# Two transformer layers: how the softmax maximum's blocks are spread over the first attention's steps at a token chunk's end

## The reference

```python
# layer 0, 16 heads of 16 features
S = jnp.einsum('hid,hjd->hij', K, Q) * SCALE
delta = idx[:, None] - idx[None, :]
decay = jnp.where(delta < 0, 0.0, -delta.astype(jnp.float32) ** ALPHA)
S = jnp.where(delta < 0, -jnp.inf, S) + decay
C = jax.nn.softmax(S, axis=-1)
attn = jnp.einsum('hij,hjd->hid', C, V)
...
x = x + ga * attention(h);  h = _layernorm(x) * (1 + cb) + sb;  x = x + gb * ffn(h)
```

## Time and profile before

| | us |
|---|---|
| median of three runs | 1557.49 |
| the profiled execution | 1556.74 |
| its span | 1554.9 |
| PE busy | 1407.1 (90%) |
| VectorE busy | 1202.4 (77%) |
| ScalarE busy | 1039.5 (67%) |
| block reductions (L1766), 832 | 914.0 |
| exponentials (L1501), 1664 | 846.2 |

### The profile page before, as it was taken

The page is one execution under the profiler, slowest core; times in us unless marked ns, Lnnn a source line. Parts: engine busy times, 40 slices in busy tenths (PEclk is TensorE's granted clock), DMA queues, the critical chain, the costliest instruction groups (busy, mean ns, idle before and its releaser), DMA issues.

```text
span 1554.9 us, 35205 instructions
## 1 busy us (share of the span) xinstructions
PE 1407.1 (90%) x13320; PEld 592.7 (38%) x13320; DVE 1202.4 (77%) x1592; ACT 1039.5 (67%) x2052; POOL 316.9 (20%) x376
## 2 busy tenths in 40 slices
PE   6878888899899998986899989999999989999998
PEld 5543333333333354442233332333333333236675
DVE  5687897898786044888899979997999779816766
ACT  2245675777688832231798978998988888984443
POOL 2401231000000032223500018300400040046225
PEclk9988999999999999996799999999999999999999
DMA  7721121011000003222200200000000000012455
GB/s 225 143 47 36 49 70 34 27 33 44 5 2 2 1 15 69 48 48 59 84 7 7 53 7 7 7 7 7 7 7 7 7 2 2 2 59 86 144 151 149
DMA packets 56867, 68.51 MB, mean 44 GB/s; under 512 B 9819, under 2 KB 52379, under 8 KB 55963
## 3 DMA queue, kind: packets, MB, share of 16 engines
q1 hardware_dynamic: 53635, 57.87, 14.2%
q0 software_dynamic: 3072, 8.39, 1.8%
HBM read 45.26 MB, written 26.74 MB: 46 GB/s over the span
## 4 chain that ended last, share of the span: by engine, by line
issue 40%; PE 33%; DVE 12%; POOL 8%; ACT 4%; DMA 3%; SPq 1%; POOLq 0%; DVEq 0%; ACTq 0%
DVE mpart L1766 8%; PE psum L1254 6%; PE psum L1229 4%; ACT probs L1501 3%; PE psum L1297 3%; PE psum L1198 3%; PE psum L1306 3%; PE psum L1325 3%; PE psum L1371 2%; PE psum L1390 1%; POOL ffn_w L972 1%; PE psum L1158 1%; DMA key_region<-in_w_up 1%; POOL key_region L984 1%; POOL key_region L986 1%
## 5 line engine op out<-in xcount | busy, mean ns | idle before, releaser
L1766 DVE TENSOR_REDUCE mpart<-psum 128x2 f32<-128x1024 f32 (+2 forms) x832 | 914.0, 1155 | 107.4 <-PE psum L1198 88.6
L1501 ACT ACTIVATE probs<-psum 128x512 f32<-128x512 f32 (+3 forms) x1664 | 846.2, 573 | 174.1 <-PE psum L1229 96.3
L1254 PE MATMUL psum<-probs,v_region 128*17 128x256 f32 (+2 forms) x6144 | 496.4, 396 | 11.6 <-ACT out_sb L1516 7.9
L1198 PE MATMUL psum<-key_region,row_region 50*128 50x512 f16 (+3 forms) x1664 | 322.8, 380 | 64.7 <-DVE mpart L1766 50.3
L1229 PE MATMUL psum<-row_region,key_region 52*128 52x512 f16 (+3 forms) x1664 | 350.9, 380 | 16.0 <-ACT probs L1501 13.3
L1229 PEld LDWEIGHTS psum<-row_region,key_region 52*128 52x128 f16 x1664 | 97.7, 93 | 354.7 <-ACT probs L1501 292.4
L1254 PEld LDWEIGHTS psum<-probs,v_region 128*17 128x17 f32 x6144 | 102.7, 95 | 206.9 <-issue 103.4
L1198 PEld LDWEIGHTS psum<-key_region,row_region 50*128 50x128 f16 x1664 | 94.5, 94 | 166.9 <-DVE mpart L1766 98.6
L928 POOL TENSOR_SCALAR vare<-mv 128x4 f32<-128x4 f32 x16 | 3.7, 232 | 646.4 <-DVE mv L1680 646.4
L1536 ACT ACTIVATE probs<-psum,gate_s 128x512 f32<-128x512 f32 (+1 forms) x24 | 16.4, 683 | 73.1 <-PE psum L1297 73.1
L1037 POOL TENSOR_TENSOR key_region<-probs,key_region 128x512 f16<-128x512 f32 (+1 forms) x24 | 28.0, 1166 | 154.1 <-ACT key_region L1545 154.0
(11 more groups left out here) (191 smaller groups left out, 1330.5 us busy)
## 6 DMA issues: line engine op xcount, KB each, us to landing
parts<-key_region SPq DMA_DIRECT2D x32, 256.0 KB, 2.7
key_region<-parts SPq DMA_DIRECT2D x48, 128.0 KB, 4.2
sorted_x<-in_zero SPq DMA_DIRECT2D x46, 128.0 KB, 2.5
key_region<-sorted_x SPq DMA_DIRECT2D x46, 128.0 KB, 2.1
sorted_y<-key_region SPq DMA_DIRECT2D x46, 128.0 KB, 1.8
row_region<-parts SPq DMA_DIRECT2D x144, 32.0 KB
key_region<-in_wmod SPq DMA_DIRECT2D x2, 1536.0 KB, 11.5
x_sb<-in_x SPq DMA_DIRECT2D x4, 512.0 KB, 8.3
```

Of the source, the lines that this page charges most:

```text
L1198: mm = pe.matmul(bank(b + par)[:, 0:w], rows[at, g, hp, r * P:(r + 1) * P], keys[at, g * HP + hp, q * CH:q * CH + w], start=True, stop=not ...
L1254: mm = pe.matmul(psum[32 * h:32 * h + VW, SUM_BANK, lo:hi], v_sb[:, jt, g * HG + h, :], probs[:, (S0[y] + s) % 2, h, lo:hi], start=(jt == ...
L1501: nc.scalar.activation(probs[:, (S0[y] + s) % 2, 2 * hp + par, off:CH], psum[:, e % 3, off:CH], ACT.Exp, scale=SCALES[y]).then_inc(s_p, 1)
L1766: V.tensor_reduce(mpart[:, n % NG, at:at + 2, q:q + 1], psum[:, b:b + 2, 0:w], AX.X, ALU.max).then_inc(drained(*item)[0], 1)
```

## The change

The factors become one dictionary for each attention. The second attention's is the old one; the first attention, which had none, gets none of its share in step 3 and half in steps 4 and 6 of units 4, 8 and 12.

```diff
--- before.py
+++ after.py
@@ -114,7 +114,7 @@
 
 def spread_blocks(y, queue):
 
-    work = [step_work(y, n, k) * (CHUNK_END.get(k, 1) if y and n and n % NG == 0 else 1) for n in range(NU) for k in range(steps_of(y, n))]
+    work = [step_work(y, n, k) * (CHUNK_END[y].get(k, 1) if n and n % NG == 0 else 1) for n in range(NU) for k in range(steps_of(y, n))]
     queue = list(queue)
     given, ready = [[] for _ in work], {}
     due = {n: sum(block_work(y, b) for b in queue if b[2] <= n) for n in range(NU)}
@@ -159,7 +159,7 @@
 
 
 
-CHUNK_END = {2: 0.5, 3: 0.0, 4: 0.5, 5: 0.5, 6: 0.25}
+CHUNK_END = ({3: 0.0, 4: 0.5, 6: 0.5}, {2: 0.5, 3: 0.0, 4: 0.5, 5: 0.5, 6: 0.25})
 RT_PIECES = 6
 DP_PIECES = 4
```

## The result

The changed kernel took 1564.12 us (median of 21 runs, 1558.32 to 1572.85), the kernel before 1557.55 (21 runs): a ratio of 1.0038, interval 1.0025 to 1.005, or 5.9 us more by the ratio. The forecast was 1555.5 with a range of 1549.5 to 1560.5. A second measurement (after_again, 12 runs against 35) gave 1.0020, 1.0004 to 1.0036, or 3 us. So the change costs 3 to 6 us by these two measurements.

What follows compares the result with a forecast made beforehand. VectorE and ScalarE were held almost in balance, with the chunk ends bound by a chain across engines. Ends give 7.5 us, landing costs 5.5: 1557.49 - 2.0 = 1555.5 us, range 1549.5 to 1560.5.

Steps and rivals of the forecast that it cites:

- The order: First attention's block table: 14 blocks leave steps 3 to 7 of units 4, 8 and 12; orders equal from step 105.
- What the ends give back: Steps 3 to 7 of units 4, 8 and 12 get shorter by 7.5 us, between 6.1 and 9.0.
- The 1.1 us for a block in step 6: Price per block from unit 12's step 6, first attention against second: 7.4 against 5.2 us for two blocks.
- The move of unit 9's transposed maximum: Unit 9's transpose of the maximum goes from unit 8's step 5 to 6: put at 0, between -1 and +1.
- What landing costs: Of 12.9 us of VectorE time leaving the ends and landing elsewhere, 5.5 us paid, kept between 0 and 12.9.
- The two unit 9 places named as free: Unit 9's steps 0 and 11 take 0.8 and 1.13 us of blocks free, since VectorE is partly idle there.
- the 6.4 us that went to steps with two or three blocks: Rest of the landing, mostly in units 5, 6, 9 and 10; with it, 5.5 us were taken as paid.
- 27 us of idle VectorE time: VectorE's idle time in the three stretches behind the ends, 6.7 + 11.5 + 8.8; basis for the landing's lower bound, nothing.
- B: Rival: step 3's hidden blocks are paid at 1.13 where they land in saturated steps; slower, 1564.3 us; chance 0.12.
- A: Rival: landing is free, VectorE's 27 us of idle time take all of it; 1550.3 us; chance 0.30.
- C: Rival: units 4 and 12 keep or get three blocks in step 5, step 6's low clock stays; 1558.5 us; chance 0.18.
- thinner ends would invite the low clock: Fear from the skill's clock rule: taking matmuls from steps where PE waits invites it; forecast read the rows the other way.

Runs made afterwards that it cites:

- after_again: The changed kernel, unaltered, measured once more with a second profile: ratio 1.0020 (1.0004 to 1.0036) against the kernel before; first attention 457.8 us.
- twice_between: Kernel before, with 8 full blocks in steps between the ends reduced twice, the second result unread: 1.0047 (1.0029 to 1.0064), 7.3 us slower.
- before_four: Kernel before, blocks pulled forward so unit 4 step 2, unit 5 step 2 and unit 6 step 1 have four: 1.0044 (1.0025 to 1.0062), 6.9 us slower.
- steps 4 and 6 alone: Kernel before with steps 4 and 6 halved and step 3 keeping its full share: 0.9973, 4.2 us faster; measured again 0.9978, 3.4 us faster.

## Why the prediction was wrong

**The order.** The table of blocks, worked out by the planner's rule, was right, and the two orders are one from step 105 on.

**What the ends give back** was forecast as 7.5 us (6.1 to 9.0) and measured as 7.1 and 8.5. The sum held, its parts did not. Step 3 gave 2.0 where 0.8 was forecast (1.3 of it in unit 4, where I had used unit 12's 0.1 for a block), and step 4 gave 2.6 where 0.9 was. Step 5 gave 4.1 us, though I had it 0.85 longer, and step 6 became longer, by 1.5 and 0.1 us in the two profiles, though I had it 5.5 shorter. That these errors cancel to the forecast sum is luck. The 1.1 us for a block in step 6 was for the most part the low clock in the window that I read it from the earlier trace rows: doubled blocks cost nothing there. I read one window at 0.77 against one at 1.00 and laid the whole difference to the blocks, though I had named the clock in the next paragraph. And a table by single steps misses what a block does to the step behind it, as unit 4's step 5 shows. The move of unit 9's transposed maximum from unit 8's step 5 to its step 6, which I had put at 0, goes with the two largest differences within the ends: unit 8's step 5 is 2.8 us shorter, and step 6, with two blocks fewer, 1.5 us longer.

**What landing costs** was forecast as 5.5 of 12.9 us and measured as 11.3 and 12.2 in the two profiles. This is the step that failed. The two unit 9 places named as free were free. Windows of the changed kernel, answering to the earlier trace rows (steps 0 and 11 of unit 9):

```profile
282.70:285.10 2.40, 2.20 (x22) 0.81 (x18) 2.09 (x2) 2.37 (x5) 0.00 (x0) 1.00 0.19 58
313.40:315.10 1.70, 1.55 (x25) 0.65 (x22) 1.23 (x1) 0.92 (x5) 0.00 (x0) 1.00 0.00 1
```

Both keep their 2.40 and 1.7 us with more of VectorE in them (1.56 to 2.09, 0.38 to 1.23), and the first steps of units 5, 8 and 11, the last of unit 11 and unit 12's steps 0 to 2 also cost 0.1 us or less in this profile. Three things were wrong. First, unit 4's step 2, which I had put among the free ones since it is long: 2.4 us for 0.6. A long step is no slack; a chain of small VectorE operations and transposes runs in it, and a block stands in that chain. Second, unit 12's step 8, which I had counted as free for 0.5 us: 0.9 us of blocks came into it, and steps 8 to 10 are 1.06 us longer, all at 1.00; two of the three have the blocks that they had before. Third, the 6.4 us that went to steps with two or three blocks I charged at less than their price, on two arguments: that shifts up and down between neighbours cancel, and that the stretches have 27 us of idle VectorE time. twice_between shows 1.06 us for each block of 1.13 there; the idle time lies in other steps (the narrow ones, and those with a transposed maximum), and the ones that I had found were already in the sum. The remainder was paid at more than its VectorE time: 11.3 less 2.4 for unit 4's step 2 and 1.1 for unit 12's steps 8 to 10 leaves 7.8 for 6.4. Part of that is the placing of unit 7's maximum, which I had put at nothing. It came from the narrow last step of unit 5 (3.0 us with it, 1.65 without) into a full one (unit 6's step 1, which also has two blocks more, 3.2 to 5.5 us). Why the rest costs more than its VectorE time stays open.

**The rivals.** B, slower because hidden blocks of step 3 are paid at the full price where they land, with 12.9 paid and 1564.3 us, was the nearest; it had a chance of 0.12. Its mechanism holds in that doubled blocks in step 3 are hidden and doubled blocks between the ends are paid, and its point of decision (more than 11 paid) was met. It isn't the whole: the counted free places were free, and others were paid above their price. That its time is met within 0.2 us is luck: its sum is 6.8 us, the first attention's profiles show 4.1 and 3.9, and the second measurement gave 3. A fell with twice_between. C is half right: unit 12 kept three blocks in step 5 (3.8 us in both) and its low clock in step 6 in one profile, not in the other. In before_four, low clock came with the added waits: 55 us of it in the first attention against 37. The Trainium skill (TensorE: Matmul & The Clock Gate, The HAM clock gate) says that activity releases the low clock and idleness brings it back; by that rule, this agrees. The changed kernel itself had 38 and 36 us, no more than before. That thinner ends would invite the low clock is not borne out: in its first profile the three ends ran at 1.00, 0.85 and 0.92, against 1.00, 0.87 and 0.92 before.

**What stays open.** How the 3 to 5.9 us of the timed runs divide between VectorE's price, the steps of four and the low clock around them. The three steps of four cost before 6.9 us when they were forced on it, yet capping them in the changed kernel gave ratios of 1.0009 and 1.0017, whose intervals hold both no change and half of the loss. Shown are these: passing over step 3 carries the loss; VectorE's time is for the most part hidden in step 3 and paid nearly whole at the eight places of twice_between; the change pays 11 to 12 us elsewhere, most of it at full clock; and unit 4's fourth block with the low clock that comes with it costs about 2 us (1.9 to 2.4 in five profiles). That full price is what sets the whole landing is argued and not shown, since steps 4 and 6 alone land 6.5 us for less. The cap's worth is undecided.

## What to carry to other kernels

An engine's idle share over a long stretch is no room for more work: look at each receiving step, and double the work in one such step if a run can be had. Before the difference of two windows is laid to the work in them, compare their granted clocks, and read the steps behind a block along with its own. When a planner's weight is taken from a step, ask first whether its work was hidden there, and list the fullest steps that the new table makes.

## What the runs showed of the hardware

The same program with the same order met the low clock at different places in different executions: unit 12's step 6 took 7.2 us at 0.76 and 5.7 at 1.00 in the changed kernel, unit 3's step 1 took 5.4 to 5.9 us at 0.72 to 0.82 in thirteen profiles and 4.4 at 1.00 in five. The low clock held for 27 to 55 us of the first attention over the eighteen profiles, and for 37 in before. Steps granted 1.00 in both profiles of one kernel agreed within 0.17 us. Adding 6.6 us of VectorE reductions in step 6 of the ends, or 8 us in step 3, changed the time by nothing that the timed runs could tell.
